# Two cross-attention layers on one core: key-projection steps between the two scores of a layer-1 pair, and copies between the row minima and exponentials

## The reference

```python
# layer 0: 32 query heads, 8 key/value heads, head width 16
q = x @ Wq + bq;  k = ctx @ Wk + bk;  v = ctx @ Wv + bv
attn = softmax(q k^T / sqrt(16) + mask)
x = layer_norm(attn v @ Wo + bo + x) * gamma + beta
# layer 1: 16 heads of width 32, keys and values from the normalised context
a = layer_norm(ctx) * ln_gamma + ln_beta
Q = x @ Wq.T;  K = a @ Wk.T;  V = a @ Wv.T
attn = softmax(where(mask, Q K^T / sqrt(32), -inf))
out = x + tanh(gate) * (attn V @ Wo.T)
```

## Time and profile before

| | |
|---|---|
| Time, median of 3 runs (lowest to highest) | 1279.66 us (1279.44 to 1281.32) |
| Profiled execution, its own time | 1280.66 us |
| Span of its instructions | 1278.9 us |
| Granted TensorE clock, mean | 0.981 of full |
| TensorE matmul busy | 1198.4 us, 94% |
| VectorE busy | 799.2 us, 62% |
| ScalarE busy | 748.8 us, 59% |
| GpSimd busy | 258.7 us, 20% |

### The profile page before, as it was taken

The page is one execution under the profiler, slowest core; times in us unless marked ns, Lnnn a source line. Parts: engine busy times, 40 slices in busy tenths (PEclk is TensorE's granted clock), DMA queues, the critical chain, the costliest instruction groups (busy, mean ns, idle before and its releaser), DMA issues.

```text
span 1278.9 us, 31973 instructions
## 1 busy us (share of the span) xinstructions
PE 1198.4 (94%) x9896; PEld 926.6 (72%) x9896; DVE 799.2 (62%) x2385; ACT 748.8 (59%) x2163; POOL 258.7 (20%) x280
## 2 busy tenths in 40 slices
PE   4899999999999999999999999999999999999976
PEld 4667786777778777777777777777777777777754
DVE  3365667666576666756666575766757576675634
ACT  3274646747475674747567574756747475674733
POOL 2222213121121311112121111312121131211200
PEclk9899999999999999999999999999999999999986
DMA  7664626447362744735274473526447363653500
GB/s 230 183 167 91 160 69 157 102 101 179 78 167 61 158 109 97 183 78 160 64 155 117 97 183 73 160 69 143 129 86 193 69 158 77 134 138 85 143 1 7
DMA packets 77821, 153.77 MB, mean 120 GB/s; under 512 B 10384, under 2 KB 47056, under 8 KB 77152
## 3 DMA queue, kind: packets, MB, share of 16 engines
q1 hardware_dynamic: 77792, 153.40, 49.5%
HBM read 113.72 MB, written 39.65 MB: 120 GB/s over the span
## 4 chain that ended last, share of the span: by engine, by line
PE 78%; issue 9%; ACT 5%; DVE 4%; DMA 2%; DVEq 0%; POOL 0%; ACTq 0%; SPq 0%; POOLq 0%
PE PJ L354 21%; PE TP L405 14%; PE SCO L391 8%; PE OA L425 5%; PE PJ L457 5%; PE SCO L634 5%; PE PJ L367 4%; PE SCO L449 4%; PE SCO L395 3%; ACT PR L980 3%; PE SCO L354 2%; DVE SCO L762 2%; PE OA L430 1%; PE SCO L621 1%; ACT PT L993 1%
## 5 line engine op out<-in xcount | busy, mean ns | idle before, releaser
L980 ACT ACTIVATE PR<-SCO,MN 100x361 f32<-100x361 f32 x768 | 425.3, 564 | 209.6 <-DVE MN L762 209.5
L762 DVE CUSTOM_DVE_ANT_0 SCO<-SCO,MK 100x361 f32<-100x361 f32 x768 | 398.7, 552 | 170.5 <-PE SCO L391 137.1
L405 PE MATMUL TP<-ident,PR 100*128 100x100 f32 x2304 | 270.1, 254 | 8.5 <-ACT PT L993 6.1
L405 PEld LDWEIGHTS TP<-ident,PR 100*128 100x128 f32 x2304 | 234.5, 143 | 59.0 <-issue 12.3
L993 ACT ACTIVATE PT<-TP 121x600 f32<-121x600 f32 x256 | 172.3, 673 | 51.1 <-PE TP L405 50.8
L980 ACT ACTIVATION_READ_ACCUMULATOR PR<-SCO,MN 100x1 f32 x768 | 156.7, 204 | 0.0
L774 DVE COPY PT<-TP 121x600 f32<-121x600 f32 x128 | 100.2, 783 | 74.9 <-PE TP L405 73.7
L391 PE MATMUL SCO<-K0S,Q0S 64*100 64x362 f32 x512 | 128.6, 407 | 7.3 <-ACT PR L980 6.3
L395 PE MATMUL SCO<-K1S,Q1S 128*100 128x362 f32 x256 | 94.2, 403 | 27.9 <-ACT PR L980 23.4
L762 DVE DVE_READ_ACCUMULATOR2_ANT MN<- 100x1 f32 x768 | 109.0, 142 | 0.0
L354 PE MATMUL PJ<-TH,WK1h 128*128 128x364 f32 x256 | 92.2, 360 | 1.2 <-DVE WK1l L836 0.9
(11 more groups left out here) (138 smaller groups left out, 1821.6 us busy)
## 6 DMA issues: line engine op xcount, KB each, us to landing
K1S<-k_scr SPq DMA_DIRECT2D x128, 364.0 KB, 6.0
k_scr<-K1HL SPq DMA_DIRECT2D x64, 364.0 KB, 2.5
Q0S<-q_scr SPq DMA_DIRECT2D x128, 100.0 KB, 4.0
K0S<-k_scr SPq DMA_DIRECT2D x64, 182.0 KB, 4.9
AT<-ctx_cols SPq DMA_DIRECT2D x16, 722.0 KB, 9.3
V<-ctx_rows SPq DMA_DIRECT2D x16, 484.0 KB
q_scr<-QHL SPq DMA_DIRECT2D x16, 400.0 KB, 2.5
k_scr<-KHL SPq DMA_DIRECT2D x32, 182.0 KB, 3.0
```

What stands on the lines that cost most here:

```text
L405: last = pe.transpose(TP[:, k % 2, c * T:(c + 1) * T], PR[0:T, k % NPR, c * SP:c * SP + P], ident[0:T, 0:T])
L762: dve.tensor_tensor_reduce(out=bank, in0=bank, in1=mask[0:T, :], scale=scale, scalar=3.4e38, op0=ALU.add, op1=ALU.min, accum_out=MN[0:T, k ...
L980: act.activation(PR[0:T, k % NPR, 0:S], SCO[0:T, k % 3, 0:S], ACT.Exp, bias=MN[0:T, k:k + 1], scale=-1.0, accum_out=SM[0:T, k:k + 1]).then ...
```

## The change

On TensorE, the key steps of pairs 17 to 23 stand between the two scores of the pair. The wait for the exponential that each score needs is now put ahead of each: S(2p) waits for map 2p-3, S(2p+1) for map 2p-2, as before. Of the twelve steps around the query product two stand ahead of it, eight behind it, and two ahead of S32 (before 3, 6 and 3).

On VectorE, the value eviction stands ahead of the first layer-1 row minimum (before behind the second). The copies of pairs 17 and 19 (at p = 20 and 22) and the two scalings of keys (at p = 18 and 21) stand between the row minima of the pair's two maps (before ahead of both). On ScalarE, the copies of pairs 16, 18 and 20 (at p = 19, 21 and 23) stand between the two exponentials (before behind both).

```diff
                 if more:
                     pe.wait_ge(v1_ev, 3 * b + 3)
-                    for i in range(3):
+                    for i in range(2):
                         keys1(b + 1, i)
...
                 if more:
-                    for i in range(3, 9):
+                    for i in range(2, 10):
                         keys1(b + 1, i)
...
-                    for i in range(9, K1_CHAIN):
+                    for i in range(10, K1_CHAIN):
                         keys1(b + 1, i)
...
-                    for k in (2 * p, 2 * p + 1):
-                        if k >= 35:
-                            pe.wait_ge(prob, NH * b + k - 2)
-                        score(b, k)
+                    if p > 17:
+                        pe.wait_ge(prob, NH * b + 2 * p - 2)
+                    score(b, 2 * p)
+                    if more and p in K1_EARLY:
+                        for i in range(*K1_EARLY[p]):
...
+                            keys1(b + 1, i)
+                    if p > 16:
+                        pe.wait_ge(prob, NH * b + 2 * p - 1)
+                    score(b, 2 * p + 1)
...
-                    if more and p in K1_EARLY:
-                        for i in range(*K1_EARLY[p]):
...
-                            keys1(b + 1, i)
                     if p >= 18:
                         transpose_probs(b, p - 2)
...
+                if more:
+                    values0(b + 1)
                 dve.wait_ge(mk1_b, b + 1)
                 for p in range(L0P, NPAIR):
+                    shift(b, 2 * p)
                     if p in (20, 22):
                         probs_out(b, p - 3)
-                    if more and p == 18:
+                    elif more and p == 18:
                         keys1_scaled(b + 1, 0)
                     elif more and p == 21:
                         keys1_scaled(b + 1, 1)
-                    for k in (2 * p, 2 * p + 1):
-                        shift(b, k)
-                    if more and p == 16:
-                        values0(b + 1)
+                    shift(b, 2 * p + 1)
...
                     exps(b, 2 * p - 2)
-                    exps(b, 2 * p - 1)
                     if p in (19, 21, 23):
                         probs_out(b, p - 3)
+                    exps(b, 2 * p - 1)
```

More of the change, by code:

```diff
@@ L660, in batch @@
                         pe.wait_ge(k1ld[1], 64 * b + 64)
-                    for k in (2 * p, 2 * p + 1):
-                        if k >= 35:
-                            pe.wait_ge(prob, NH * b + k - 2)
-                        score(b, k)
+                    if p > 17:
[3 more added lines that the diff above has]
+                        for i in range(*K1_EARLY[p]):
+                            if i == 3 * C:
+                                pe.wait_ge(v0_ev, b + 2)
+                            elif i == 6 * C:
+                                pe.wait_ge(k1_f, 4 * b + 5)
+                            keys1(b + 1, i)
+                    if p > 16:
+                        pe.wait_ge(prob, NH * b + 2 * p - 1)
+                    score(b, 2 * p + 1)
                     if p == 23:
```

## The result

The changed kernel took 1272.60 us in the median of 6 runs (1268.31 to 1275.06), the kernel before 1280.09 us in the 6 runs beside it (1279.15 to 1281.32). The ratio is 0.9938, 95% interval [0.9923, 0.9953]: 6 to 10 us faster. The forecast was 1268 us, some 12 us faster. The profiled execution took 1274.04 us, its span was 1272.2 us (before 1278.9 us).

What follows compares the result with a forecast made beforehand. TensorE bounds the kernel, with holes in the layer-1 pairs from three score banks and a single transpose buffer. 15 x (0.15 + 0.7) less 1.0 gives 11.75 us off, so 1268 us; range 1261 to 1277 us.

Steps and rivals of the forecast that it cites:

- Query product: Per batch with a successor, one key step fewer ahead starts it 0.15 us earlier (bounds 0 and 0.17).
- Value eviction: On VectorE ahead of the first layer-1 minimum, it fills 0.67 us of idle time and costs nothing (at worst 0.1 us).
- Pairs 17 to 19: Layer-1 pairs whose key steps fill waits for exponentials; S40 comes 0.75 us earlier, at 651.4 instead of 652.15 us.
- Pairs 20 and 22: Layer-1 pairs with VectorE's copy behind a minimum; each takes 2.4 us, not 1.70 us, giving back 0.7 us twice.
- Pair 21: Layer-1 pair with ScalarE's copy C18 between exponentials; takes 1.6 us, not 2.37 us, with exponential 41 just in time.
- The stretch: S32 to the next batch's S0, 14.92 us before; forecast 0.7 us shorter (0.2 to 0.9), about 14.2 us.
- the layout: Layer-1 pairs' timeline built from hand-over times in the trace, before and after; it shrinks S32 to S0 by 0.67 us.
- the last batch: No key steps there and half clock; T18 0.85 us later, twice, ScalarE's copies give some back: 1.0 us slower (0.4 to 1.8).
- The much faster rival: Layer-1 copies C17 and C19 don't wait behind minima; next S0 1.84 us earlier, 30 us gained, 1250 us; chance 0.12.
- The slower rival: VectorE's layer-1 copies late, ScalarE's no earlier; S32 to S0 0.39 us longer, 4.6 us slower, 1284 us; chance 0.10.
- The third, holes that only move: Layer-1 gains fully given back in later pairs; only the query product's 0.15 us remains, 1278.4 us; chance 0.16.
- the sum's own bounds: Whole-kernel gain limits from the terms' bounds: 15 x (0 + 0.2) - 1.8 = 1.2 us to 15.7 us.

Runs made afterwards that it cites:

- only the split: The kernel before with only the twelve key steps around the query product split 2, 8 and 2; 1281.49 us, ratio 0.9991.
- only the key steps: The changed kernel with both engines' copies placed as in the kernel before, keeping key steps, query product steps and early value eviction; 1275.18 us, ratio 0.9942.
- the fastest version: The changed kernel with VectorE's copies of pairs 17 and 19 put back ahead of both row minima, in all batches; 1254.27 us, ratio 0.9778.

## Why the prediction was right, and where it was off

Query product: right. 0.15 us was forecast; 0.14 us earlier against S0, 0.03 us of it lost ahead of S32.

Value eviction: right that it costs nothing where it now stands: S32's minimum starts 0.57 us behind S32 (641.82 us), as it did with 0.56 us before (646.26 us). "Costs nothing and frees VectorE" undersells it: left in its old place, under key steps that have moved ahead of S35, it costs 0.66 us per batch.

Pairs 17 to 19: S32 to S40 was forecast 0.75 us shorter, and is 5.75 us instead of 6.45 us, 0.70 us.

Pairs 20 and 22: 2.4 us forecast, 2.40 and 2.42 us measured, with C17 1.05 us behind S40 to the hundredth. Pair 21: 1.6 us forecast, 1.52 us measured, and exponential 41 is the one without slack.

The stretch: 0.7 us less was forecast, 0.71 us measured. This is not errors that cancel: counted from S32, the layout put S36, S37, T16, S40, T18, S42, T19 and S44 at 2.54, 3.44, 3.63, 5.7, 7.6, 8.1, 9.17 and 9.7 us, and they stand at 2.53, 3.44, 3.69, 5.75, 7.64, 8.15, 9.14 and 9.68 us. A score directly in front of transposes, for which the prediction had no row, took 0.17 to 0.26 us to the first of them. With the query product a loop batch was to win 0.85 us and wins 0.84 us. Batch 0 wins less, so that 12.19 us were won ahead of the last batch and not 12.75 us.

The scalings of keys at p = 18 and 21, which also moved between the minima, have no term in the prediction, and no run puts them back alone.

The much faster rival was ruled out for the right reason, and its price stands confirmed from the other side: with VectorE's copies taken out from behind the minima the stretch shrinks by 1.82 us against the kernel before, where the layout had 1.84 us, and the time comes to 1254.3 us, where 1250 us was given. The slower rival, too, is a real state of this code, from which ScalarE's earlier copies keep it. That it met its 1284 us with 1284.7 us is in part luck: it had the stretch 0.39 us longer, and it is 0.20 us longer. The third, holes that only move, is nearly what one sees when only key steps or only ScalarE's copies are moved.

The range given, 1261 to 1277 us, is not the one that the sum's own bounds make, 1264.0 to 1278.5 us, and the prediction gives no reason for the difference. The measured 1272.60 us lies in both.

The step that was off is a term of the sum, the last batch: 1.0 us was taken (0.4 to 1.8), and in the profiles it lost 4.3 to 5.1 us. The layer-1 pairs themselves lost 1.29 us (15.28 to 16.57 us), inside those bounds and for the reason given: pairs 20 and 22 are 0.91 and 0.90 us longer, forecast 0.85 us twice; pairs 19 and 21 are 0.33 and 0.21 us shorter, forecast 0.2 us three times (the third brought nothing ahead of T21). But another 3.0 us went at a lower granted clock in the same batch, 1.13 us between S0 and the query product and 1.88 us behind T21, which the prediction had taken as unchanged. The 12.2 us won less the 4.3 to 5.1 us lost leave some 7 to 8 us, which is the measured gain. The two executions at 0.979 and 0.980 of the full clock, 1269.06 and 1268.31 us, stand at the forecast.

What lowers that clock is open. The order of the last batch's instructions alone does not set it. From S0 to the query product that order is one and the same in all thirteen profiles, and took 50.47 to 53.48 us. Behind it, too, several kernels share it on TensorE, VectorE, ScalarE and GpSimd. With the copies as in the kernel before, the pairs took 15.28 to 15.29 us in four profiles, but the whole last batch 93.5 and 92.7 us (the kernel before), 94.4 us (only the split) and 96.9 us (only the key steps). With the copies as in the changed kernel the batch took 97.8 us three times, and 95.7 us in the run with the late eviction. With the copies as in the fastest version the pairs took 14.7 us in four profiles, and the part behind T21 took 20.15, 20.5 and 20.24 us in three, but 17.55 us in the run with the key steps behind both scores. The fastest version and that run, from T21 to the end:

```profile
1233.65:1253.80 20.15, 13.27 (x122) 9.75 (x118) 3.71 (x8) 2.15 (x6) 0.00 (x0) 0.67 0.04 10
1257.85:1275.40 17.55, 10.64 (x122) 7.80 (x118) 3.70 (x8) 2.15 (x6) 0.00 (x0) 0.86 0.04 12
```

The same 122 products follow the same pairs, and 2.6 us lie between them with the granted clock. So the order alone does not fix these 3.0 us: the 1.13 us of them ahead of the query product fall in a part that no edit touched. Whether the new order has a share in the rest is not shown; the part behind T21 took 19.2 to 19.4 us in the four profiles with the changed kernel's copies, and 17.3, 17.3, 17.5 and 18.8 us in the four with the old ones. The loss repeats in three profiles of the changed kernel, so it is not bare chance either. What it follows no run here shows.

## What to carry to other kernels

In a pipeline through a small ring, list for each buffer what releases it and where that stands in its engine's queue: an operation whose input is ready should not stand behind one that waits for something just issued. VectorE's copies, put behind a minimum of a score only then issued, cost 0.73 and 0.83 us in their pairs and 1.11 us a batch net. ScalarE's copies, taken out from behind an exponential that could wait, won 0.91 us a batch in the changed kernel. Moves that each win little because they uncover the other's wait must be tried together, and each half of an edit apart: here the change without the new place of VectorE's two copies won 27 us, and that place took 18 us back. When single profiles are compared, look at the stages apart: here the last batch alone took 4 to 5 us of the 12 us won ahead of it.

## What the runs showed of the hardware

Within one execution the stretches of the changed kernel's loop batches agree to 0.05 us, and whole loop batches to 0.08 us. The hand-overs between the engines, from which the layout was made, came back after the change, in the rows of pairs 20 and 21 above: row minimum 0.59 us behind its score (0.60 us in the prediction), transposes 0.83 us behind VectorE's copy (0.84) and 0.72 us behind ScalarE's (0.72), score 0.70 us behind the exponential that frees its bank (0.70). With them the layout of eight pairs hit the separate steps to 0.06 us.

Around the loop nothing is so steady: the start varied between 110.8 and 114.3 us over thirteen profiles, with a granted clock of 0.91 in the first profile of the kernel before (111.66 us) and 0.87 in its second (114.31 us). The last batch took between 92.7 and 97.8 us. At its end the same products took 17.3 us at a granted clock of 0.87 and 20.15 us at 0.67.
